# Two constant TensorE products behind each step of a lone pair of images, and more at two other places

## The reference

```
def step(w, b):
    def f(carry, inp):
        nxt = inp + _conv1d(carry, w, b)
        return (nxt, nxt)
```

## The kernel before, in words

| beats | lone pair | what else goes on |
|---|---|---|
| 65 to 71 | 0 | softmax of image 3, its convolution starts |
| 120 to 130 | 0 | pair 1 arrives: group norm and scaling |
| 254-255, 385-386, 817-818, 948-949 | 1, 0, 1, 0 | turn between two scans |
| 510 to 562 | 1 | pair 0 between its layers; swap copies of pair 1 on VectorE (L1393) |
| 641 to 693 | 0 | pair 1 between its layers |
| 1073 to 1203 | 1 | pair 0 is done and leaves: additions (L382) on VectorE in its first 64 beats and on GpSimd, writes to `flat_rows`, tokens read back (L500), statistics from beat 1163 on |

## Time and profile before

### The profile page before, as it was taken

The page is one execution under the profiler, slowest core; times in us unless marked ns, Lnnn a source line. Parts: engine busy times, 40 slices in busy tenths (PEclk is TensorE's granted clock), DMA queues, the critical chain, the costliest instruction groups (busy, mean ns, idle before and its releaser), DMA issues.

```text
span 2996.9 us, 47545 instructions
## 1 busy us (share of the span) xinstructions
PE 2689.8 (90%) x18080; PEld 2308.4 (77%) x18080; DVE 1608.3 (54%) x4237; ACT 1013.2 (34%) x2620; POOL 389.0 (13%) x442
## 2 busy tenths in 40 slices
PE   2989999999999989999998898899999987764896
PEld 2989859744997569999997697799999976651343
DVE  3323233223333267777778676577775554246865
ACT  3433353444333434344442241243444421111221
POOL 1000000003000056000004204100000033313330
PEclk9999999999998989999997596699999975556998
DMA  8830000021000140000003204200000023308242
GB/s 154 147 56 1 1 0 1 1 44 41 1 1 1 43 92 16 2 2 2 1 2 100 69 2 116 33 2 2 2 2 1 1 58 90 105 15 251 57 140 84
DMA packets 53091, 130.28 MB, mean 43 GB/s; under 512 B 9472, under 2 KB 34400, under 8 KB 45248
## 3 DMA queue, kind: packets, MB, share of 16 engines
q1 hardware_dynamic: 51808, 126.50, 17.8%
q10 hardware_dynamic: 928, 0.76, 0.1%
q0 software_dynamic: 128, 0.01, 0.0%
HBM read 76.91 MB, written 50.33 MB: 42 GB/s over the span
## 4 chain that ended last, share of the span: by engine, by line
PE 86%; DVE 7%; ACT 3%; issue 2%; DMA 1%; ACTq 0%; POOL 0%; SPq 0%; DVEq 0%; POOLq 0%
PE bank L1030 19%; PE bank L1033 16%; PE bank L1031 16%; PE bank L923 13%; PE bank L982 11%; PE bank L941 3%; PE bank L928 3%; ACT image L782 2%; DVE work L382 2%; PE bank L1163 2%; PE bank L1105 1%; DMA work<-in_x 1%; DVE stats L1186 1%; PE bank L1096 1%; DVE image L1393 1%
## 5 line engine op out<-in xcount | busy, mean ns | idle before, releaser
L1030 PE MATMUL bank<-image,scan_wt 112*112 112x128 f32 x4064 | 885.4, 301 | 125.4 <-ACT image L782 124.8
L782 ACT COPY image<-bank 112x128 f32<-112x128 f32 x2032 | 546.4, 269 | 1300.0 <-PE bank L1033 1225.9
L1380 DVE TENSOR_SCALAR bank<-image,scan_bias 112x128 f32<-112x128 f32 x2032 | 713.1, 354 | 496.0 <-ACT image L782 455.2
L1031 PE MATMUL bank<-image,scan_wt 112*112 112x126 f32 x4064 | 826.4, 287 | 0.0
L1033 PE MATMUL bank<-image,scan_wt 112*112 112x126 f32 x4064 | 826.2, 286 | 0.0
L1030 PEld LDWEIGHTS bank<-image,scan_wt 112*112 112x112 f32 x4064 | 602.5, 188 | 227.6 <-ACT image L782 199.0
L1031 PEld LDWEIGHTS bank<-image,scan_wt 112*112 112x112 f32 x4064 | 634.6, 190 | 0.0
L1033 PEld LDWEIGHTS bank<-image,scan_wt 112*112 112x112 f32 x4064 | 631.7, 191 | 0.0
L923 PE MATMUL bank<-work 112*128 112x192 f32 x2304 | 421.3, 331 | 13.5 <-issue 13.5
L728 ACT ACTIVATE work<-image,gn_shift,gn_scale 48x567 f32<-48x567 f32 (+3 forms) x384 | 335.8, 899 | 263.9 <-PE bank L928 146.8
L923 PEld LDWEIGHTS bank<-work 112*128 112x128 f32 x2304 | 373.9, 192 | 16.2 <-issue 15.9
(11 more groups left out here) (139 smaller groups left out, 1565.5 us busy)
## 6 DMA issues: line engine op xcount, KB each, us to landing
work<-saved SPq DMA_DIRECT2D x64, 384.0 KB, 7.2
saved<-image SPq DMA_DIRECT2D x32, 384.0 KB, 5.9
flat_rows<-work SPq DMA_DIRECT2D x32, 384.0 KB, 4.7
image<-flat_rows SPq DMA_DIRECT2D x4, 3072.0 KB, 15.8
out<-image SPq DMA_DIRECT2D x8, 1536.0 KB, 9.1
band<-in_x SPq DMA_DIRECT2D x16, 384.0 KB, 5.5
work<-in_x SPq DMA_DIRECT2D x16, 384.0 KB, 5.6
saved<-image SPq DMA_DIRECT2D x4, 1536.0 KB, 23.6
```

What stands on the lines that cost most here:

```text
L782: nc.scalar.copy(line(g, along_w, at), state_bank(g, done)).then_inc(s_state[g], 1)
L1030: mm(dst, wt[:, 1], src, start=False, stop=False, skip_group_check=True)
L1031: mm(dst[:, 1:J2, :], wt[:, 0], src[:, 0:J2 - 1, :], start=False, stop=False, skip_group_check=True)
L1380: v.tensor_scalar(state_bank(g, done), line(g, along_w, src), scan_bias[:, 3 * layer + kind:3 * layer + kind + 1], None, ALU.add).then_inc ...
```

## The change

A helper `keep_busy` is added: it issues `count` products of `group_half` (112x112) by 128 columns of the identity into a spare bank, with no semaphore. Nobody reads the result. It is called at three places of TensorE's program.

1. In the beat loop: two products behind the steps of each beat in which not both pairs have a step (256 beats, 512 products), into bank 4.
2. In the bare softmax of image 3 (seven beats): two behind each of the first five steps, none behind the sixth, four behind the seventh, into bank 0.
3. After the last beat: TensorE waits until `s_res` is 14, that is until VectorE has finished six of its last eight parts, and does 24.

```diff
+            def keep_busy(count, spare=bank[4]):
+
+                for i in range(count):
+                    mm(spare[0:P, 0:2 * J2], group_half[:, :], identp[0:P, 0:2 * J2], start=True, stop=True)
+
...
             for i in range(7):
                 next_step()
+                if i != 5:
+                    keep_busy(2 if i < 5 else 4, bank[0])
                 if i == 1:
                     key_norms(3)
...
             while beat < BEATS:
+                steps = 0
                 for g in range(2):
                     if beat >= g * LEAD and beat < g * LEAD + END:
                         step(g, beat)
+                        steps += moment(g, beat)[2] < STEPS
+                if steps < 2:
+                    keep_busy(2)
...
             pe.wait_ge(s_gate_const, 16 * 4)
+            pe.wait_ge(s_res, 4 * PER - 2)
+            keep_busy(24)
```

## The result

The changed kernel takes 2870.72 us, the median of four runs (2859.21 to 2880.54), beside 3006.56 us (3002.57 to 3013.22) of the kernel before: ratio 0.9545, 95% interval 0.9505 to 0.9585. The forecast was 2874, range 2850 to 2902. The profiled execution took 2871.79 us with a span of 2870.0; before it was 2998.7 with 2996.9, so the two traces differ by 126.9 us.

A forecast was written before the change was run, and what follows sets the result against it. TensorE, too little fed by a lone pair, falls to half clock, costing 0.70 us a beat. The terms sum to 130.8 us gained, taken from the 3004.8 us median: 2874 us, range 2850 to 2902.

The forecast's parts named there:

- Lone beats: Beats with one pair stepping: two products fit into 1.32 us at full clock; at half each costs 0.11 us more.
- C: Last long half-clock stretch, 253.4 us, 125 steps: 87.5 us less 9.6 for contention with GpSimd's additions, gain 78.
- B: Half-clock stretch of 102.4 us, 51 steps without swap copies, VectorE below 1.32 us a beat: gain 33 us.
- A: Half-clock stretch of 102.4 us, 49 steps, in three parts gaining 1, 15.1 (middle, VectorE-bound) and 4.5 us: 20.6.
- The sums behind the products and the spells: At the norms: group sums wait behind two products, -1 us; half-clock spells after stalls, -3.6 us.
- First 11 lone beats: A 17.0 us spell with 8 steps at half clock: gain 2.5 us, reduced by later collisions with GpSimd work.
- Softmax: Bare softmax of image 3, 17.1 us at half clock: gain 2 us, bounds -2 and +8.
- 24 products: Ahead of the channel stage: done 6 us or more before it, clock fallen again; cost 0, gain counted 0.
- full rate (1): VectorE absorbs swaps and contention, 225 steps of A, B and C at 1.32 us: 161 gained, 2844 us; chance 0.10.
- oscillation (2): Each contended beat in C, A and at stalls lets the clock fall: gain 101, 2904 us; chance 0.14.
- "no effect" (4): Idle gaps, not the share of work, lower the clock, and gaps at each step's end remain: 3005 us; chance 0.02.
- The third: Clock stays at half although TensorE is solid; 225 steps lose 0.11 us each: 3030 us; chance 0.03.

The follow-up runs named there:

- e2: Changed kernel without the products of the beat loop's lone beats, those of the softmax and the 24 kept: 3005.53 us, ratio 1.0001.
- e7: Changed kernel with four products of 2 columns per lone beat in place of two of 128: 3183.44 us, ratio 1.0595.
- e9: Changed kernel without VectorE's statistics of pair 0 between its two layers, except the last one: 2877.01 us in its one run.
- e6: Changed kernel with group norm sums issued ahead of the products and six products in the three beats from the first sums: 2872.14 us, ratio 0.9564.
- e1: Changed kernel without the softmax products and the 24 ahead of the channel stage, lone-beat products kept: 2872.83 us, ratio 0.9552.
- e5: Changed kernel with 24 and 15 more products after the 24, released by VectorE's seventh and eighth parts: 2877.30 us, ratio 0.9569.
- e11: Changed kernel with VectorE's second addition chunk eight beats earlier, inside GpSimd's row of additions: 2873.71 us, ratio 0.9567.

## Why the prediction came out right, step by step

- **What bounds.** Right. TensorE's clock cost the lone pair 0.70 us a beat, and without the products it still does (e2).
- **Lone beats.** Right: two products fit into the gap at full clock (1.33 us a beat), four don't (1.52). The step "PE is solid, so the clock rises" held with products of 128 columns; with products of two, TensorE was as solid by the profile's count and the clock stayed at half (e7). The forecast took a busy TensorE for enough.
- **C, 78 us:** 82.2 measured. The contended beats are 1.64 us as forecast, but the contention cost 4.0 us (88.5 us for the first 64 beats, less 64 of 1.32) and not 9.6: behind the first of GpSimd's parts none to three beats a part are lengthened, not 3.8. Against it, the norm at beat 1188 costs 2.2 us beyond its beats, 0.7 more than before. The tokens landed 20 us after their request at the latest, and the first reader came at 28.
- **B, 33 us:** 33.7. Right in an execution like the profiled one. That GpSimd's row now reaches into VectorE's second chunk was seen ("they start a chunk later, so nothing is late"), but not that a single addition could then wait 9 us: where it does, B is worth 24.
- **A, 20.6 us:** 13.7, the term with the largest miss. Its middle is bound by VectorE as forecast (e9), at 1.51 and not 1.44 us a beat; with its first two beats, which fall into a spell of half clock, it is 1.52. One pair of beats on VectorE in the changed kernel:

```profile
1655.08 0.35 DVE L1393 TENSOR_SCALAR bank<-image,scan_bias 112x128 f32<-112x128 f32 x1
1655.46 0.69 DVE L1199 BATCH_NORM_STATS2 stats<-image 112x6 f32<-112x512 f32 x1
1656.17 0.24 DVE L1406 COPY image<-image 48x128 f32<-48x128 f32 x1
1656.51 0.24 DVE L1406 COPY image<-work 48x128 f32<-48x128 f32 x1
1656.79 0.35 DVE L1393 TENSOR_SCALAR bank<-image,scan_bias 112x128 f32<-112x128 f32 x1
1657.17 0.69 DVE L1199 BATCH_NORM_STATS2 stats<-image 112x6 f32<-112x512 f32 x1
1657.88 0.29 DVE L1406 COPY work<-image 48x128 f32<-48x128 f32 x1
1658.09 0.34 DVE L1393 TENSOR_SCALAR bank<-image,scan_bias 112x128 f32<-112x128 f32 x1
```

  From preload to preload it is 1.71 and 1.30 us, 1.505 on average. Its busy time is 1.42 of that; the pauses, 0.10 before the second copy for one, are more than I allowed. That is 12.9 us instead of 15.1. The last third brought 1.0 instead of 4.5: VectorE waits less at the norm (1.8 us for 3.4 in the earlier trace rows), but the stall lets the clock fall, as this timeline of the changed kernel shows, where passes of 0.47 us become 0.77:

```profile
1678.01 0.60 PE L1052 MATMUL bank<-identp,group_half 112*112 112x128 f32 x4
...
1678.45 0.27 PE L898 MATMUL bank<-mean_var,group_half 112*112 112x2 f32 x2
...
1678.75 0.16 DVE L1210 COPY gn_mean<-bank 112x2 f32<-112x2 f32 x1 [1.84 <-PE bank L898]
...
1680.52 0.27 ACT L782 COPY image<-bank 112x128 f32<-112x128 f32 x1 [3.30 <-DVE bank L1393]
...
1680.84 0.77 PE L1030 MATMUL bank<-image,scan_wt 112*112 112x128 f32 x2 [2.12 <-ACT image L782]
```

  The spell lasts from 1680.8 to 1691.0, ten us and not the 6.8 that I took as the longest of the short spells of before; the trace of before has one of 10.2 us too, at 2950.9 in the channel stage. e6 gets up to 2.7 us of it back, and where the spell is 3.4 us (e1, e5, e11) the last third is 1.3 to 1.8 us shorter. The sums behind the products and the spells had terms of their own (-1, -3.6); with A's third of them the miss is some 5 us. The first part brought nothing instead of 1.
- **First 11 lone beats, 2.5 us:** nothing, 0.1 lost. They and the five beats behind them gained 4.0, and beats 136 to 138 gave 4.1 back: GpSimd's row of fills, 11 us long in both kernels, now reaches into them, and VectorE's swap copies beside it take 1.1 to 1.6 us instead of some 0.25. The mechanism was in the forecast, its size too small.
- **Softmax, 2 us:** 3.1 in the profile, but not attributable to the products (e1, e2). **Turns, -0.7:** -0.9, all of it in two of the four. **24 products, 0:** as forecast the clock had fallen again before the stage; 8.6 us of it at half clock instead of 4.7, and the last segment 0.5 us shorter, within its variation. The prediction weighed the advice of the Trainium skill, "TensorE: Matmul & The Clock Gate", section "Why this matters for your kernels", to warm up with matmuls before what is measured. Here it paid only in the stage's first products, and only where the filler reached up to them (e5: 1.04 instead of 1.95 us), not in the kernel's time.

The terms measured are 13.7 + 33.7 + 82.2 + 3.1 - 0.1 - 0.9 = 131.7, the forecast's sum 130.8. A's shortfall and C's surplus cancelled. The total was closer than its terms deserved: that is luck, though the mechanism was right. Of the rivals, full rate (1) fails at A's middle, oscillation (2) at 1.00 of granted clock in B and C of the changed kernel, and "no effect" (4) at the result itself; e7 shows besides that the half clock needs no gaps. The third, a clock that stays at half though TensorE is solid, is what e7 does, at 0.74 us a beat instead of the 0.11 of wide products.

## What to carry to other kernels

Where a chain with short products leaves TensorE at half clock, try unused wide products queued behind each step; size them so that they end when the next operand arrives. Here two of 128 columns held the full clock, one did in an undisturbed stretch, and four cost 23 us in C alone. Such a filler helps only where TensorE's time is on the path: price each stretch by the engine that comes next (VectorE in A), and look for the rows of another engine's work that the faster pace runs into. The filler that ended 8.4 us ahead of the channel stage did nothing for it.

## What the runs showed of the hardware beyond what was expected

- **A TensorE without idle time in the profile is not enough for the full clock.** In e7 weight loads and products of two columns filled 131.10 of 132.50 us and the granted clock was at half throughout; half-clock time over its trace was 794.8 us, more than the 607.9 of the kernel before.
- **Weight loads follow the granted clock.** The same load of 112 columns, at half clock in e7 and at full in the changed kernel (ns min/median/max):

```profile
L1084 PEld LDWEIGHTS bank<-identp,group_half x340: 307/307/311, 1879.8 to 1999.9; 112*112 112x112 f32 x170
```
```profile
L1052 PEld LDWEIGHTS bank<-identp,group_half x207: 173/174/178, 2480.2 to 2550.0; 112*112 112x112 f32 x104
```

  From load to load it is 0.19 us at half clock. The loads of the steps themselves agree: those of L1030 take 0.17 us at full clock (before, 1300 to 1400) and 0.26 to 0.31 at half (before, 2560 to 2680). The Trainium skill, "TensorE: Matmul & The Clock Gate", in the section "LDWEIGHTS (loading the stationary operand)", gives a time by the columns alone, which for 112 is an estimated 0.093 us whatever the clock; these runs disagree at half clock.
- **An addition of VectorE can last until a whole row of GpSimd's has ended.** The 9.67 us of the addition in e5 end with a row of GpSimd additions of 1.2 us each (nine of them took 11.05 us); some eight of them ran meanwhile. In other executions the same addition took 1.1 to 1.5 us. The Trainium skill, "SBUF — State Buffer", in the section "SBUF: two separate sides", describes the port that the two share as a lock which the first one keeps for one whole instruction. That fits the usual 1.5 us beside GpSimd instead of 0.68; it doesn't say why VectorE should be passed over for a whole row, and no run here explains it.
